# A two-layer attention and mixture kernel: the first norm applied by ScalarE, two narrow matmul groups made 128 columns wide, and a new order of each engine's work within a body

## The chip, the cores and the metric

One NeuronCore of a Trainium2 chip runs the kernel. The metric is the device time in microseconds (us) of one execution; the kernel before took 1501.69 us (median of 3 runs, 1501.0 to 1501.98). A core has five engines with an instruction stream each, which meet only through semaphores: TensorE (PE; its weight loads are PEld), VectorE (DVE), ScalarE (ACT), GpSimd (POOL) and SyncE (SP), which here only issues DMAs.

## The reference

The input is x of 16 batches x 512 tokens x 128 features, in float32. In short:

```python
x = x + linear_attention(norm(x))        # "layer 1": q, k, v of 16 heads of 8; Chebyshev terms of order 1 to 5 of
                                         # clipped q, k; running sums over tokens; numerator / denominator; W_out
y = norm(x)
y = y + causal_softmax_attention(norm(y) * g1 + b1)     # "layer 2"
y = y + top2_of_8_experts(norm(y) * g2 + b2)            # gate logits = h @ gate_W + gate_b
out = x + y
norm(x) = (x - mean) / sqrt(var + 1e-5)                 # over the 128 features of a token
den = (Tq.sum(-1) * k_beta).sum(orders)                 # one denominator per token and head
```

## The kernel before, in words

A batch (512 tokens, four tiles of 128) is one unit of work. Layer 1, layer 2's projections, the row maxima of the softmax, the scores with the values, and the gate are five stages of a software pipeline. `pipelined` (L306) calls a `body` 21 times on each engine, with up to six batches in flight: f (first norm, projections and Chebyshev terms), h (running sums, denominators, output of layer 1), g (projections of layer 2), m (row maxima), b (scores, exponentials, values) and t (gate and dispatch of rows to the experts). Body -5 has only f, body -4 f and h, body -3 adds g, body -2 adds m, body -1 adds b, and bodies 0 to 10 have all six. Then the stages fall away again (f first, then h), until body 15 has t alone. Behind the last body come 39 blocks of expert work (L1589 to L1599), which the change doesn't touch.

Within a body every engine's order is written out by hand. Each of DVE, ACT and PE runs through 129 numbered slots. Long runs of equal work have lists of slots: row maxima on PE (`MAX_PE`, 44 in a body, `maximum`, L1362) and on DVE (`MAX_DVE`, L583), scores on PE (`SCORES_PE`, 48, L1400) and their exponentials on ACT (`EXPS_ACT`, L966), value matmuls (`VALUES_PE`, 12, L1419). Every other step has one slot (`at(n, stage)`). A slot is only a place in that engine's own order; it is no time. POOL's order stands in its own `body` (L1188) without slots.

Two rings tie the engines: a score matmul may run at most two ahead of the exponentials (L1407), and a maximum matmul at most two ahead of DVE's reductions (L1370). All waits are in order, so what stands behind a waiting instruction on its engine waits too.

The steps that the change touches:

- **The first norm.** `stats0` (DVE, slot 0, L506) writes mean and variance; `ln_rsqrt("a", f)` (POOL, L1193 calling L412) makes 1/sqrt; `apply0` (DVE, slot 23, L461) writes `hn = (x - mean) * rstd` as four 128x128 instructions; `turn_h` (PE, slot 61) transposes it; `take_h` (ACT, slot 40) copies it to `hT`; `project_k` and `project_q` (PE, slots 68 and 69, both on L1277) use it.
- **The other norms.** ACT applies them with scale and shift (`ln_shift`, L455): `apply3` (slot 10), `apply1` (73), `apply2` (77). For those POOL makes a shift, -mean * rstd, in two more steps (L427, L428) and a last one (L444).
- **The denominators.** `denominators` (PE, slot 32, L1310): four matmuls of float32 with a 128x128 stationary operand and 16 moving columns. `invert_den` on DVE (slot 18) adds epsilon and inverts, and `turn_rden` (PE, slot 47) transposes.
- **The gate.** `gate` (PE, slot 33, L1467): four matmuls of float32 with 8 moving columns, then `gate_top` (DVE, slot 25), `gate_exp` (ACT, 28), `gate_weights` (DVE, 28), `ranks` (PE, 58), `slots` (DVE, 34), and POOL's eight indirect DMAs (`dispatch`, L1176).
- **Layer 2's projections.** `turn_ln` (PE, slot 43), `affine1` (ACT, 26), `project_q2` (PE, 51, L1351), `project_k2` (PE, 52, L1354), `project_v2` (55, L1359).
- `copy_rows` (ACT, slot 12, L993) copies the normed rows; `set_tables` (DVE, body -5 only) fills constant tables.

The profile counts one float32 matmul as two PE instructions.

Of the kernel before, what the change touches and what calls it, by code (L numbers as in the profile page):

```python
# [22 lines left out]
ALU = mybir.AluOpType  # L23
# [88 lines left out]
def block_kernel(nc, x, consts, cols, row_biases, w_in, w_out, wq, wk, wv, wp, gate_w, ew1, ew2, eb2, out):  # L112
    with ExitStack() as ctx:
# [90 lines left out]
        for c in "amb":  # L204
# [84 lines left out]
        MAX_PE = (1, 2, 7, 8, 11, 13, 20, 23, 38, 41, 44, 49, 53, 54, 57, 60, 62, 65, 67, 71, 73, 75, 77, 79, 85, 88, 89, 93, 94, 99, 102,  # L289
                  106, 107, 110, 112, 114, 116, 117, 119, 120, 122, 123, 124, 126)  # L290
        SCORES_PE = (0, 5, 6, 10, 12, 14, 16, 17, 18, 19, 21, 24, 26, 27, 29, 30, 31, 34, 36, 37, 39, 40, 42, 46, 48, 50, 56, 59, 64, 66,
                     70, 78, 80, 84, 86, 90, 92, 95, 97, 98, 101, 104, 105, 108, 109, 111, 113, 115)
        VALUES_PE = (15, 22, 28, 35, 45, 63, 76, 87, 96, 103, 118, 121)
        MAX_DVE = (1, 2, 6, 7, 9, 11, 19, 20, 22, 24, 26, 27, 29, 30, 31, 32, 33, 35, 38, 40, 42, 44, 47, 48, 51, 54, 55, 58, 59, 61, 62,
                   64, 65, 66, 67, 68, 69, 70, 71, 72, 73, 74, 75, 77)
        EXPS_ACT = (0, 1, 2, 3, 4, 5, 6, 7, 8, 9, 11, 13, 15, 16, 18, 19, 20, 21, 22, 23, 24, 25, 27, 29, 31, 32, 37, 39, 42, 45, 49, 54,
                    56, 58, 59, 61, 62, 63, 65, 66, 67, 68, 69, 70, 71, 72, 74, 75)
        LEAVE_ACT = (17, 43, 64)
        SPLIT_DVE, SPLIT_ACT = (6, 10, 15, 20), (8, 9, 11, 15, 30, 32, 34, 36)
# [112 lines left out]
        def ln_rsqrt(c, n):  # L412
# [43 lines left out]

        def ln_apply(c, n, src, dst):
            k = norm[c]
            nc.vector.wait_ge(k["ready"], n + 1)
            for t in range(QT):  # L460
                nc.vector.tensor_scalar(dst(t), src(t), k["mv"][:, t, 0:1], k["rstd"][:, t:t + 1],  # L461
                                        ALU.subtract, ALU.mult).then_inc(k["out"], 1)
# [3 lines left out]
        def _(dve):  # L466
# [42 lines left out]

            def apply0(f):  # L510
                ln_apply("a", f, tile_of(f), lambda t: hn[:, t, :])
# [160 lines left out]
            def body(t, b, m, g, h, f, p):  # L672

                for n in range(SLOTS):
# [7 lines left out]
                    if at(3, t):  # L682
                        x2(t)
# [6 lines left out]
                    if at(10, h):  # L690
                        times_v(h, (0, 1))
                    if at(12, h):
                        sum_kv(h, (0,))
                    if at(13, h):
# [9 lines left out]
                    if at(18, h):  # L704
                        invert_den(h)
                    if at(21, h):
                        sum_kv(h, (4,))
                    if at(23, f):
                        apply0(f)
                        if f == 0:  # L710
                            set_tables()
# [6 lines left out]
                    if at(36, g):  # L718
                        third_part(g, 2, kf, ks)
                    if at(37, g):  # L720
                        third_part(g, 1, qf, qs)
                    if at(39, f):
                        clip(f, kx, W.hk_ev, W.k_clip)
                    if at(41, f):
                        clip(f, qx, W.hq_ev, W.q_clip)
                    if at(43, b):
# [899 lines left out]
```

## Time and profile before

| | |
|---|---|
| median of 3 runs | 1501.69 us |
| the profiled execution's own time | 1503.87 us |
| its span (first to last instruction) | 1501.6 us, 27731 instructions |
| mean granted TensorE clock | 0.907 |
| busy: PE, DVE, ACT, POOL | 1261.9, 1152.0, 912.0, 847.7 us |
| chain that ended last | PE 64%, DVE 15%, ACT 8%, issue 5%, DMA 3%, POOL 3% |
| of it `hn` by DVE, L461 | 3% |
| largest waits | ACT L972 for PE L1415 199.0 us; PEld L1412 for ACT L972 123.7 us; DVE L587 for PE L1375 95.5 us |

The profiled execution took 2.3 us more than its span, and 2.2 us more than the median. The span falls into four parts: five bodies that fill the pipeline (to about 231 us), the eleven full bodies (to about 928 us, some 63 us each), five bodies that drain it (to about 1180 us) and the expert blocks. "Granted clock" is the share of TensorE's full clock of 2.4 GHz that the throttle let through; its two levels are 1.00 and 0.50. "Idle before, with a releaser" means that the engine did nothing for that long and that the named instruction's semaphore ended it.

### The profile page before, as it was taken

Reading aid. Unit: us, or ns where it says so; the run is one execution under the profiler, and the core shown is the slowest. Engines: PE = TensorE matmul, PEld = TensorE weight load, DVE = VectorE, ACT = ScalarE, POOL = GpSimd, SP = SyncE. Lnnn points to the kernel's source line nnn. Section 1 sums busy time; section 2 is a strip of 40 time slices with the busy share of each in tenths; the row PEclk is TensorE's granted clock in tenths of the full one; section 3 lists DMA queues with packets and bytes.
Section 4 is the critical chain, followed back from the end, with each engine's and each line's share of the span. In section 5 each row is a group of like instructions: output and inputs, shape, how many; then the busy total and the mean of one; then the engine's idle time right before and its main releaser. Section 6 shows DMA issues by size and latency. Waiting matters only on the chain.

```text
span 1501.6 us, 27731 instructions
## 1 busy us (share of the span) xinstructions
PE 1261.9 (84%) x8819; PEld 734.1 (49%) x8819; DVE 1152.0 (77%) x2622; ACT 912.0 (61%) x1795; POOL 847.7 (56%) x1077
## 2 busy tenths in 40 slices
PE   3466898999999999899998999988886399999970
PEld 1233254554545445454454544544343288888750
DVE  5658888888988888888988888856541588888765
ACT  1233376676756766567665766674564488888760
POOL 5776545667666676666767666532213246666570
PEclk8567799999999999999999999998998599999995
DMA  3032121422224222242321413223033212222238
GB/s 98 0 84 64 22 76 22 111 64 53 75 41 108 72 51 72 44 108 64 60 72 37 97 37 83 72 44 94 23 121 141 75 51 76 86 80 79 67 118 352
DMA packets 79344, 116.22 MB, mean 77 GB/s; under 512 B 15396, under 2 KB 61496, under 8 KB 74976
## 3 DMA queue, kind: packets, MB, share of 16 engines
q1 hardware_dynamic: 65888, 92.41, 23.7%
q0 software_dynamic: 9088, 17.33, 3.4%
q10 hardware_dynamic: 4224, 4.72, 0.9%
q8 instruction: 71, 1.16, 0.3%
q14 instruction: 73, 0.60, 0.1%
HBM read 58.29 MB, written 57.43 MB: 77 GB/s over the span
## 4 chain that ended last, share of the span: by engine, by line
PE 64%; DVE 15%; ACT 8%; issue 5%; DMA 3%; POOL 3%; another core or an unknown queue 1%; SPq 0%; POOLq 0%; DVEq 0%; ACTq 0%
PE back L1432 8%; PE scores L1412 8%; PE maxima L1373 8%; DVE nm L587 7%; PE front L1565 7%; PE back L1577 6%; PE front L1302 4%; PE maxima L1375 3%; DVE hn L461 3%; ACT pr L972 3%; PE front L1277 3%; PE scores L1415 2%; PE back L1252 2%; ACT rows L455 2%; DMA stack<-pairs 2%
## 5 line engine op out<-in xcount | busy, mean ns | idle before, releaser
L972 ACT ACTIVATE pr<-scores 128x384 f32<-128x384 f32 (+1 forms) x768 | 382.2, 525 | 232.0 <-PE scores L1415 199.0
L587 DVE TENSOR_REDUCE nm<-maxima 128x1 f32<-128x384 f32 (+3 forms) x704 | 426.7, 635 | 107.7 <-PE maxima L1375 95.5
L1412 PE MATMUL scores<-stack 98*128 98x512 bf16 (+3 forms) x1024 | 271.0, 314 | 32.7 <-ACT pr L972 29.8
L1373 PE MATMUL maxima<-stack 96*128 96x128 bf16 (+3 forms) x1024 | 258.0, 313 | 41.7 <-DVE nm L587 39.6
L1176 POOL DMA_INDIRECT xg<-rows,sloti x128 | 133.3, 1042 | 111.2 <-DVE sloti L657 71.4
L1412 PEld LDWEIGHTS scores<-stack 98*128 98x128 bf16 x1024 | 94.0, 102 | 197.6 <-ACT pr L972 123.7
L1415 PE MATMUL scores<-maskB,identb 128*128 128x128 bf16 (+1 forms) x768 | 189.0, 246 | 0.0
L1432 PE MATMUL back<-pr,vaug 128*9 128x512 f32 (+3 forms) x2048 | 182.5, 452 | 0.0
L1375 PE MATMUL maxima<-maskA,identb 128*128 128x128 bf16 (+2 forms) x704 | 177.4, 252 | 0.0
L1373 PEld LDWEIGHTS maxima<-stack 96*128 96x128 bf16 x1024 | 90.1, 100 | 170.1 <-DVE nm L587 81.3
L1241 POOL DMA_INDIRECT pairs<-xs x104 | 105.8, 1017 | 92.4 <-DVE xs L822 65.0
L1565 PE MATMUL front<-h_first,w_now 128*128 128x512 f32 x312 | 129.2, 415 | 6.2 <-ACT xs L1111 3.0
L1111 ACT ACTIVATE xs<-front,b1p 128x512 f32<-128x512 f32 x156 | 107.3, 688 | 32.2 <-PE front L1565 20.6
L1146 POOL TENSOR_TENSOR kv<-F,kv 128x512 f32<-128x512 f32 x80 | 107.1, 1360 | 12.4 <-DVE kv L541 12.2
L1137 POOL TENSOR_SCALAR F<-F 128x512 f32<-128x512 f32 x32 | 56.7, 1772 | 72.7 <-DVE F L520 71.2
L1577 PE MATMUL back<-hid_first,w_now 128*128 128x512 f32 x312 | 97.1, 393 | 0.0
L541 DVE TENSOR_TENSOR_SCAN kv<-one,front 128x512 f32<-128x512 f32 x80 | 93.5, 1201 | 0.0
L815 DVE TENSOR_TENSOR hid_second<-xs,hid_first 128x512 fp32r<-128x512 f32 x99 | 68.0, 687 | 28.2 <-ACT hid_first L1092 26.5
L1157 POOL TENSOR_TENSOR kv<-kv 128x512 f32<-128x512 f32 x64 | 81.0, 1275 | 3.8 <-POOL kv L1157 0.4
L1415 PEld LDWEIGHTS scores<-maskB,identb 128*128 128x128 bf16 x768 | 77.3, 101 | 11.4 <-issue 4.0
L1092 ACT ACTIVATE hid_first<-xs 128x512 fp32r<-128x512 f32 x117 | 74.0, 633 | 3.7
L1167 POOL TENSOR_TENSOR qf<-qf,qs 128x512 f32<-128x512 f32 x16 | 18.5, 1156 | 100.2 <-ACT qs L922 100.2
(222 smaller groups left out, 2542.5 us busy)
## 6 DMA issues: line engine op xcount, KB each, us to landing
stack<-spread SPq DMA_DIRECT2D x64, 384.0 KB
spread<-qs SPq DMA_DIRECT2D x96, 128.0 KB
spread<-ks SPq DMA_DIRECT2D x96, 128.0 KB
xs<-xg SPq DMA_DIRECT2D x39, 272.0 KB
stack<-pairs SPq DMA_DIRECT2D x8, 1024.0 KB
xg<-xs SPq DMA_DIRECT2D x17, 272.0 KB
xs<-in_x SPq DMA_DIRECT2D x16, 256.0 KB
acc<-xs SPq DMA_DIRECT2D x16, 256.0 KB, 2.3
```

Source lines behind the costliest of these rows:

```text
L587: v.tensor_reduce(nm[:, h:h + heads, t], ring(n)[:, 0:heads * (t + 1) * P].rearrange("p (h n) -> p h n", h=heads), AX.X, ALU.max, negate=T ...
L972: a.activation(pr[:, n % PR, 0:width], ringE[n % 2][:, 0:width], ACT.Exp).then_inc(W.exp_ready, 1)
L1111: a.activation(gel[n % GS], (X, Y)[n % 2][:, :], ACT.Gelu, bias=b1p[:, bass.ds(ahead * HC + c, 1)]).then_inc(W.mid_ready, 1)
L1146: g_.tensor_tensor(kv[:, p, :], qx[p], kv[:, p, :], ALU.mult).then_inc(W.qk_prod, 1)
L1176: g_.indirect_dma_start(xg[:, :], bass.IndirectOffsetOnAxis(sloti[:, i, q:q + 1], 0), rows[:, i, q, :], None).then_inc(W.dispatched, 16)
L1373: k.matmul(ring(n)[:, at:at + (t + 1) * P], qst[p][0:MROW, h, t * P:(t + 1) * P], kst[p][0:MROW, h, 0:(t + 1) * P], start=(j == 0), stop=T ...
L1375: k.matmul(ring(n)[:, 0:heads * (t + 1) * P].rearrange("p (h n) -> p h n", h=heads)[:, :, t * P:(t + 1) * P], identb[:, :], maskA[:, 0:hea ...
L1412: k.matmul(dst[:, at:at + T - t * P], kst[p][0:MROW + 2, h, t * P:(t + 1) * P], qst[p][0:MROW + 2, h, t * P:T], start=(t == tiles[0]), sto ...
L1415: k.matmul(dst[:, 0:2 * P * many].rearrange("p (i n) -> p i n", i=many)[:, :, 0:P], identb[:, :], maskB[:, 0:many * P].rearrange("p (i n) ...
L1432: last = k.matmul(V[32 * i:32 * i + DH + 1, t * P:T], vaug[:, b % VR, t, 4 * (s_ // 3) + i, :], pr[:, (4 * s_ + i) % PR, at:at + T - t * P ...
L1565: last = k.matmul((X, Y)[n % 2][:, :], w_now[:, i % 2, wi, c * P:(c + 1) * P], h2p[hi][:, i % 2, :], start=(j == 0), stop=(j == len(TERMS3 ...
L1577: last = k.matmul((Z, V)[i % 2][:, :], w_now[:, i % 2, 2 + wi, c * P:(c + 1) * P], (hidh, hidl)[hi][i % 2 * HC + c], start=(c == 0 and j = ...
```

## The change

DVE no longer applies the first norm; ACT does, by `ln_shift`, for which POOL makes the shift in norm "a" too. The denominators and the gate write 128 columns per tile, of which the first 16 or 8 are used (each tile overwrites the surplus of the one before). `project_k`'s wait is on another semaphore where g is absent. All slots are chosen anew, and on POOL `dispatch(t, 0, (3,))` stands ahead of the even orders of q, and `ln_rsqrt("m", h)` behind `dispatch(t, 1, (1,))`.

```diff
-        LEAVE_ACT = (17, 43, 64)
-        SPLIT_DVE, SPLIT_ACT = (6, 10, 15, 20), (8, 9, 11, 15, 30, 32, 34, 36)
+        LEAVE_ACT = (20, 45, 66)
+        SPLIT_DVE, SPLIT_ACT = (6, 10, 15, 20), (8, 9, 11, 32, 35, 37, 39, 41)
...
-            steps = first + (shifted if c != "a" else []) + (second if c == "m" else [])
+            steps = first + shifted + (second if c == "m" else [])
...
-                if c != "a" and i + 1 == len(first) + len(shifted):
+                if i + 1 == len(first) + len(shifted):
                     g.tensor_tensor(shift, minus, rstd, ALU.mult).then_inc(k["ready"], 1)
-            if c == "a":
-                g.tensor_tensor(rstd, y0, a, ALU.mult).then_inc(k["ready"], 1)
...
DVE body
                     if at(0, f):
                         stats0(f)
+                        if f == 0:
+                            set_tables()
-                    if at(3, t):
+                    if at(1, t):
                         x2(t)
...
-                    if at(21, h):
-                        sum_kv(h, (4,))
-                    if at(23, f):
-                        apply0(f)
+                    if at(18, h):
+                        sum_kv(h, (4,))
+                    if at(19, h):
+                        invert_den(h)
...
-                    if at(28, t):
+                    if at(27, t):
                         gate_weights(t)
-                    if at(34, t):
+                    if at(32, t):
                         slots(t)
...
ACT body
+            def apply0(f):
+                act.wait_ge(norm["a"]["ready"], f + 1)
+                ln_shift("a", tile_of(f), lambda t: hn[:, t, :], False)
...
-                    if at(12, t):
-                        copy_rows(t)
-                    if at(14, t):
+                    if at(13, t):
                         affine2(t)
+                    if at(16, f):
+                        apply0(f)
-                    if at(26, g):
+                    if at(28, h):
+                        take_rden(h)
+                    if at(29, g):
                         affine1(g, t)
-                    if at(28, t):
+                    if at(31, t):
+                        copy_rows(t)
+                    if at(33, t):
                         gate_exp(t)
-                    if at(30, h):
-                        take_rden(h)
...
-                    if at(60, m):
+                    if at(64, m):
                         put_maxima(m, p, 0)
-                    if at(73, h):
+                    if at(77, h):
                         apply1(h)
-                    if at(77, h):
+                    if at(78, h):
                         apply2(h, g)
-                    if at(80, m):
+                    if at(81, m):
                         put_maxima(m, p, 1)
...
POOL body
                     dispatch(t, 0, (2,))
+                    dispatch(t, 0, (3,))
                 if f is not None:
                     even_orders(f, qx, W.q_t35, W.q_t24)
-                if t is not None:
-                    dispatch(t, 0, (3,))
-                if h is not None:
-                    ln_rsqrt("m", h)
                 if t is not None:
                     dispatch(t, 1, (0,))
                     dispatch(t, 1, (1,))
                 if h is not None:
+                    ln_rsqrt("m", h)
                     keep_residual(h)
...
PE body
-                    last = k.matmul(X[:, t * H:(t + 1) * H], ksum[:, t * P:(t + 1) * P], cst[:, C_WS:C_WS + H],
+                    last = k.matmul(X[:, t * H:t * H + P], ksum[:, t * P:(t + 1) * P], cst[:, C_WS:C_WS + P],
                                     start=True, stop=True)
...
-                    last = k.matmul(Z[:, t * E:(t + 1) * E], h2[:, t * P:(t + 1) * P], gw_sb[:, :], start=True, stop=True)
+                    last = k.matmul(Z[:, t * E:t * E + P].rearrange("p (i n) -> p i n", n=E), h2[:, t * P:(t + 1) * P],
+                                    gw_sb[:, :].unsqueeze(1).to_broadcast((P, P // E, E)), start=True, stop=True)
...
-                    if at(33, t):
+                    if at(37, t):
                         gate(t)
-                    if at(43, g):
+                    if at(42, g):
                         turn_ln(g, h)
-                    if at(47, h):
+                    if at(44, h):
                         turn_rden(h)
...
-                    if at(68, f):
+                    if at(66, f):
                         project_k(f, h, g)
-                    if at(69, f):
+                    if at(71, f):
                         project_q(f)
-                    if at(74, f):
+                    if at(77, f):
                         project_v(f)
...
```

## Rows read from the trace of the kernel before

**Rows 1.** Busy us per engine, granted clock: the sum over the eleven bodies, 246.9 to 943.8.
```profile
sum 696.90, PE 654.59 PEld 346.26 DVE 605.09 ACT 461.17 POOL 466.20; mean PE 59.51 PEld 31.48 DVE 55.01 ACT 41.92 POOL 42.38
```
**Rows 2.** Timeline of PE (start us, us, instructions): denominators and the next project_k.
```profile
246.87 1.01 PE L1310 MATMUL front<-cst,ksum 128*128 128x16 f32 x8
...
625.04 1.01 PE L1310 MATMUL front<-cst,ksum 128*128 128x16 f32 x8
...
643.90 1.93 PE L1277 MATMUL front<-hT,w_in_sb 128*128 128x512 f32 x4
...
834.71 1.93 PE L1277 MATMUL front<-hT,w_in_sb 128*128 128x512 f32 x4
...
879.11 1.01 PE L1310 MATMUL front<-cst,ksum 128*128 128x16 f32 x8
...
943.84 1.04 PE L1310 MATMUL front<-cst,ksum 128*128 128x16 f32 x8
```
**Rows 3.** The chain that ended last, in order of time, 624 to 644.
```profile
629.72 3.08 DVE hn L461 x4
...
635.53 1.81 PE front L1351 x2
637.34 1.48 PE front L1354 x2
```
**Rows 4.** Timeline of PE: waits in that stretch, and layer 2's projections in four bodies.
```profile
258.20 1.07 PE L1351 MATMUL front<-lnT,wq_sb 128*128 128x512 f32 x2
...
573.63 1.07 PE L1351 MATMUL front<-lnT,wq_sb 128*128 128x512 f32 x2
574.54 1.02 PE L1354 MATMUL front<-lnT,wk_sb 128*128 128x512 f32 x2
...
633.45 0.40 PE L1373 MATMUL maxima<-stack 96*128 96x128 bf16 x4 [0.66 <-DVE nm L587]
...
634.91 0.51 PE L1412 MATMUL scores<-stack 98*128 98x512 bf16 x1 [0.84 <-ACT pr L972]
...
953.48 1.07 PE L1351 MATMUL front<-lnT,wq_sb 128*128 128x512 f32 x2
```
**Rows 5.** Busy time by stretch: PE, PEld, DVE, ACT, POOL, then PE's granted clock.
```profile
559.90:563.40 3.50, 2.94 (x35) 1.87 (x26) 2.42 (x4) 2.84 (x6) 3.50 (x4) 0.99 0.00 0
563.40:570.20 6.80, 6.80 (x33) 3.49 (x34) 4.67 (x8) 2.39 (x5) 6.58 (x6) 0.50 0.00 0
...
635.00:638.40 3.40, 3.40 (x6) 1.40 (x6) 2.04 (x10) 1.77 (x4) 0.00 (x0) 0.51 0.01 2
```
**Rows 6.** Groups of instructions by form: count, busy us, mean ns of one, idle before.
```profile
L461 DVE TENSOR_SCALAR hn<-xs,mva,rstda 128x128 f32<-128x128 f32 x64 | 52.2, 875 | 5.5 <-POOL rstda L446 5.5
...
L455 ACT ACTIVATE rows<-x2t,moreb,rstdb 128x128 f32<-128x128 f32 x64 | 26.2, 482 | 5.6 <-POOL moreb L444 5.6
...
L993 ACT ACTIVATE rows<-rows 128x512 f32<-128x512 f32 x16 | 9.9, 620 | 0.0
```
**Rows 7.** The same view: matmuls of 16 and of 128 columns on 128x128 stationary operands.
```profile
L1310 PE MATMUL front<-cst,ksum 128*128 128x16 f32 x128 | 18.8, 281 | 22.0 <-DVE kv L541 22.0
...
L1359 PE MATMUL front<-wv_sb,lnT 128*128 128x128 f32 x128 | 17.7, 284 | 0.0
```
**Rows 8.** Timeline of ACT just behind the denominators of body 6.
```profile
627.22 0.49 ACT L972 ACTIVATE pr<-scores 128x384 f32<-128x384 f32 x1 [1.49 <-PE scores L1415]
```
**Rows 9.** Timeline of POOL: last steps of norm "b", and of norm "a" behind it.
```profile
617.60 0.20 POOL L427 TENSOR_TENSOR rstdb<-lnvb 128x4 f32<-128x4 f32 x1
...
618.34 0.20 POOL L444 TENSOR_TENSOR moreb<-moreb,rstdb 128x4 f32<-128x4 f32 x1
...
621.85 0.20 POOL L446 TENSOR_TENSOR rstda<-lnva 128x4 f32<-128x4 f32 x1
```
**Rows 10.** Timeline of PE in bodies -4 and -2: waits that end with or behind hn.
```profile
45.62 1.11 PE L1252 MATMUL front<-cst,hn 128*128 128x128 f32 x4 [5.58 <-DVE hn L461]
...
131.68 0.61 PE L1373 MATMUL maxima<-stack 96*128 96x128 bf16 x4 [3.54 <-DVE nm L587]
```

More of the change, by code:

```diff
@@ L455, in ln_shift @@
                 nc.scalar.activation(dst(t), src(t), ACT.Identity, bias=bias[:, t:t + 1], scale=scale[:, t:t + 1]).then_inc(k["out"], 1)
[L457 to L462, printed above, removed]
         @block.vector
@@ L691, in body @@
                         times_v(h, (0, 1))
+                    if at(11, h):
+                        sum_kv(h, (0,))
                     if at(12, h):
-                        sum_kv(h, (0,))
-                    if at(13, h):
                         sum_kv(h, (1,))
@@ L1039, in body @@
                         take_k(f, h)
-                    if at(46, f):
+                    if at(48, f):
                         take_q(f, h)
-                    if at(47, f):
+                    if at(49, f):
                         square(f, kx, W.k_clip, W.k_sq)
-                    if at(48, f):
+                    if at(50, f):
                         square2(f, kx, W.k_sq)
-                    if at(50, f):
+                    if at(51, f):
                         square3(f, kx, W.k_sq)
-                    if at(51, f):
-                        take_v(f, h)
                     if at(52, f):
                         square(f, qx, W.q_clip, W.q_sq)
-                    if at(53, f):
+                    if at(54, f):
+                        take_v(f, h)
+                    if at(55, f):
                         square2(f, qx, W.q_sq)
-                    if at(55, f):
+                    if at(57, f):
                         square3(f, qx, W.q_sq)
-                    if at(57, m):
+                    if at(59, m):
                         max_parts(m, 0)
-                    if at(60, m):
+                    if at(64, m):
                         put_maxima(m, p, 0)
-                    if at(73, h):
-                        apply1(h)
                     if at(76, b):
@@ L1064, in body @@
                     if at(77, h):
+                        apply1(h)
+                    if at(78, h):
                         apply2(h, g)
-                    if at(78, m):
+                    if at(79, m):
                         max_parts(m, 1)
-                    if at(79, b):
+                    if at(80, b):
                         take_y(b)
-                    if at(80, m):
+                    if at(81, m):
                         put_maxima(m, p, 1)
@@ L1494, in body @@
                         head_sums(h, kx, X, W.k_t24, W.k_t35, W.ks_mm, W.x1_ready, h)
-                    if at(9, h):
+                    if at(10, h):
                         head_sums(h, qx, Y, W.q_t24, W.q_t35, W.qs_mm, *((W.x2_ready, t + 1) if t is not None else (W.outT_ready, h)))
-                    if at(25, t):
+                    if at(24, t):
                         turn_x2(t)
@@ L1526, in body @@
                         spread_rden(h, g, f)
-                    if at(82, b):
+                    if at(82, m):
+                        turn_maxima(m, b, 0)
+                    if at(86, b):
                         turn_back(b, 1, t)
-                    if at(83, m):
-                        turn_maxima(m, b, 0)
-                    if at(91, h):
+                    if at(93, h):
                         output1(h, g, f)
-                    if at(100, b):
+                    if at(102, b):
                         turn_back(b, 2, t)
-                    if at(125, b):
+                    if at(124, b):
                         turn_back(b, 3, t)
```

82 lines of the change are left out of this document (39 added, 43 removed).

## The prediction

> **What bounds the kernel now.** I read four views in turn. First the busy time by stretch: in the eleven bodies between the first and the last denominators with all stages around them, PE is busy 654.59 of 696.90 us and DVE 605.09, ACT and POOL only 461.17 and 466.20 [rows 1]. PE is the bound, and DVE stands close behind it. Second, PE's timeline at two marks of a body, the start of the denominators and that of `project_k`. From `project_k` to the next denominators PE takes 44.40 us (879.11 less 834.71), and in the other bodies the same to 0.1. The mean period is (943.84 - 246.87) / 11 = 63.36 us [rows 2]. So the whole variation, and as I shall argue most of the loss, lies in the stretch from denominators to `project_k`: 63.36 - 44.40 = 18.96 us on average. Third, the chain of waits in one such stretch: `hn` on DVE stands in it with 3.08 us in one piece, and behind it come `project_q2` and `project_k2` with 1.81 and 1.48 us [rows 3]. Fourth, the clock. At the full clock such a pair takes 0.91 us from start to start [rows 4]; in this body both ran at 0.51 of the clock, the level of 1.2 GHz [rows 5].
>
> **The stretch without its losses.** In body 6 it took 643.90 - 625.04 = 18.86 us [rows 2]. PE waited 0.66 us for DVE's reduction, which stood behind `hn`, and 0.84 us for ACT [rows 4]; ACT had to sit out DVE's gate work, which stood behind `hn` too. The two pairs cost 1.81 + 1.48 - 2 x 0.91 = 1.47 us too much through the clock [rows 3, 4]. What PE needs by itself is 18.86 - 1.50 - 1.47 = 15.9 us. In body 5 the clock fell right behind denominators and gate, for 6.8 us, without much waiting before it: PE was busy 2.94 of the 3.50 us ahead [rows 5], with the narrow groups as its last work. So the loss has two sources, a wait behind `hn` or narrow matmuls ahead of a fall, and the change goes at both.
>
> **`hn` leaves DVE.** Four instructions a body, 64 x 875 ns = 52.2 us in all [rows 6]. The cleanest look at its worth is the first body without f: there `project_q2` starts 953.48 - 943.84 = 9.64 us behind the denominators, in the body at 246.87, with gate and DVE's `hn` and the same single fall of the clock, 11.33 us [rows 2, 4]. That is 1.7 us a body from DVE alone, though 3.1 us leave it: PE takes over as bound for the rest.
>
> **`hn` comes to ACT.** 4 x 482 ns = 1.9 us a body at most, and `copy_rows`, 0.62 us, moves from ahead of it to a later slot [rows 6]. So ACT's work ahead of the denominators grows by 1.3 us net, with exponentials behind it for which PE's scores wait. Behind the denominators ACT was idle for 1.49 us in one piece [rows 8], which is the cover. The ring of two scores lets part of it through: between nothing and 1.3 us a body I take 0.3, near the lower end because ACT's cover is larger than the growth. PE's `turn_h` is late in the order and has no reason to wait.
>
> **POOL's shift.** Norm "a" gets two more small steps; for norm "b" they take 618.34 - 617.60 = 0.74 us [rows 9]. The result comes at 622.05 + 0.74 = 622.8 instead. ACT reaches slot 16 at about that time, so I charge nothing in full bodies; POOL's products behind it start 0.7 us later, hidden by POOL's idle third [rows 1]. Without that cover it would be 0.7 us a body.
>
> **Denominators and gate wide.** Eight float32 matmuls a body. A group of 16 columns has a mean of 281 ns an instruction, one of 128 columns 284 [rows 7]; 16 instructions a body cost 0.05 us. The Trainium skill, in "TensorE: Matmul & The Clock Gate", Back-to-back issue gap, has the gap grow with the moving columns, at the full clock by 112 / 2.4 = 47 ns for 112 columns more. An estimate from that page is 0.75 us a body, some 9 us in all, and the forecast would be as much higher; the rows show instead that these groups take what their weights take. What the width gives is the clock. If it stays up behind the groups, the stretch loses its second source too. The trace of before can't show this. Its bounds are nothing, and the whole difference between a stretch of 18.96 - 1.7 = 17.3 and one of 15.9 us.
>
> **The moves.** The last running sum (DVE) goes ahead of `invert_den`, into DVE's wait for PE; `turn_rden` and ACT's copy are needed only at `project_q2` and later. The gate moves four slots back on PE and `gate_exp` five on ACT, so that exponentials stand no more behind DVE's gate work. Maxima and scores are interleaved otherwise; I take their effect as zero between -1 and +1 us a body. `ln_rsqrt("m")` goes behind two more indirect DMAs of POOL, and both `apply1` and `apply2` behind the third evacuation on ACT, before `take_y`; the two small DMAs of `put_maxima` move back by a few slots and are wanted only by the next body's scores. `set_tables` goes ahead of POOL's result, where DVE idled.
>
> **The sum.** For a body I take 15.9 us plus 0.5 for waits that remain or come new = 16.4 us, so 18.96 - 16.4 = 2.6 less, and 0.3 back for ACT: 2.3 us. Twelve bodies (the eleven, and body -1) give 27.6. Filling the pipeline: in body -4 PE stood 5.58 us for `hn`, in body -2 3.54 us for the reduction behind it [rows 10]; I take 4.0 and 3.5, less 0.7 for POOL's steps in body -3 and 1.2 for these and ACT's slower `hn` in body -5: 5.6. The body at 943.84 has the narrow groups alone: 0.8. Together 34 us. Against the profiled execution, 1503.9, that is 1469.9; against the median of the runs, which is 2.2 lower, **1468 us**.
>
> **Rivals.**
> - *The clock stays as it is*, only DVE's share comes: 12 x (1.7 - 0.3) + 5.6 = 22 us, **1479**. For it: PE was hardly idle before the fall at 563.4 [rows 5], so it isn't plain that wider matmuls help. The Trainium skill, same page, Part 1, ties the throttle to idleness of PE; by that rule widening busy work would do nothing, and this rival would be the result. The row of 2.94 busy of 3.50 with a fall behind it speaks against idleness as the only cause. Chance 0.22.
> - *The rest of the body gets shorter too.* PE is idle or its releases late for (696.90 - 654.59) / 11 = 3.8 us a body [rows 1], some 2.3 of it outside the stretch. If the new order takes 1.2 of that and my charges of 0.3 fall away, 12 x 1.5 = 18 us more: **1450**. Chance 0.15.
> - *Slower: ACT waits for POOL in `apply0`.* Slot 16 stands ahead of exponentials, and these ahead of PE's scores. POOL gets to norm "a" only behind norm "b" [rows 9], and to that behind the indirect DMAs of the body before, of which two more now hold up `ln_rsqrt("m")` and with it the residual. If the result comes w us later than ACT is there, PE loses w - 1.5, ACT's cover taken off [rows 8]. Against a gain of 2.3 us it decides from w = 3.8 a body; at w = 5 twelve bodies lose 14 us net, less 6 of the filling: **1510**. Against it: POOL's busy share is only 67% [rows 1], and `stats0` stays at slot 0. Chance 0.08.
> - *Nothing:* a wait of 2 to 3 us takes the place of `hn` (ACT's tail, two norms ahead of `take_y`): 1501. Chance 0.05.
>
> **How the numbers follow.** The forecast has 0.50, from 1458 to 1478 (2.3 us a body with 0.8 either way). With the first rival and most of the second the range is 1450 to 1490. A measurement of this kernel can tell about 0.2%, 3 us. Faster by more: 0.50 + 0.22 + 0.15 = 0.87; within: 0.05; slower: 0.08.
>
> **What would show it.** Periods between denominators of 60.5 to 61.5 us; denominators to `project_k` in 16 to 17 us; no stretch at the half clock right behind the denominators; L461 gone from DVE, 64 more of L455 on ACT at 0.48 us; `turn_h` of body -4 some 4 us earlier. It would be wrong if the half clock shows up as often, if `project_k` to denominators takes more than 45 us, or if ACT stands idle for POOL's L444 in full bodies.

## The result, and the profile after

| | before | changed |
|---|---|---|
| median of the runs | 1501.35 us (4 runs) | 1484.1 us (1480.95 to 1487.06, 4 runs) |
| ratio, 95% interval | | 0.9889 (0.9864 to 0.9913) |
| span of the profiled execution | 1501.6 us | 1481.8 us |
| granted clock, whole span | 0.907 | 0.922 |

The change gained 17 us; I had forecast 33 to 34. The range held it, the number did not. A second measurement, in a later set of runs, gave 1484.55 us and a ratio of 0.9903 (0.9867 to 0.9939). The page of the changed kernel (share of the span and count behind each busy time; then the chain that ended last):

```profile
span 1481.8 us, 27795 instructions
...
PE 1243.5 (84%) x8819; PEld 730.9 (49%) x8819; DVE 1107.9 (75%) x2558; ACT 942.3 (64%) x1859; POOL 864.5 (58%) x1109
...
PE 61%; POOL 9%; issue 9%; ACT 9%; DVE 7%; DMA 3%; another core or an unknown queue 1%; POOLq 0%; SPq 0%; ACTq 0%; DVEq 0%
```

DVE's share of the chain fell from 15% to 7%. The marks of the body [rows 2], on PE's timeline of the changed kernel (start, duration, instructions):

```profile
180.92 1.71 PE L1300 MATMUL front<-cst,ksum 128*128 128x128 f32 x8
...
241.46 1.11 PE L1300 MATMUL front<-cst,ksum 128*128 128x128 f32 x8
...
608.47 1.11 PE L1300 MATMUL front<-cst,ksum 128*128 128x128 f32 x8
...
623.11 1.07 PE L1267 MATMUL front<-hT,w_in_sb 128*128 128x512 f32 x2
...
915.00 1.13 PE L1300 MATMUL front<-cst,ksum 128*128 128x128 f32 x8 [0.40 <-DVE kv L529]
```

The mean period is (915.00 - 241.46) / 11 = 61.23 us, in place of 63.36. In body 6 the stretch from denominators to `project_k` took 623.11 - 608.47 = 14.64 us, in place of 18.86; the rest of the body, from `project_k` to the next denominators, grew from 44.4 us to 46.6 (61.23 - 14.64). The windows (PE, PEld, DVE, ACT, POOL busy, then the granted clock) of the first 3.4 us of that stretch, and of one of the three short falls that are left in the full bodies [rows 5 in the kernel before]:

```profile
608.40:611.80 3.40, 3.40 (x30) 2.18 (x29) 1.96 (x5) 2.55 (x6) 3.40 (x4) 1.00 0.02 5
...
484.60:488.00 3.40, 3.06 (x14) 2.38 (x14) 1.31 (x3) 1.98 (x5) 3.40 (x4) 0.56 0.00 0
```

The groups by form [rows 6 and 7]: the new `hn` on ACT, the denominators and the gate.

```profile
L453 ACT ACTIVATE hn<-xs,morea,rstda 128x128 f32<-128x128 f32 x64 | 26.2, 482 | 36.8 <-POOL morea L444 36.8
...
L1300 PE MATMUL front<-cst,ksum 128*128 128x128 f32 x128 | 23.8, 345 | 19.2 <-DVE kv L529 19.2
...
L1457 PE MATMUL back<-gw_sb,lnT 128*128 128x128 f32 x128 | 18.7, 291 | 0.9 <-ACT lnT L974 0.9
```

ACT waited 36.8 us for POOL's L444, all of it in bodies -5 to -2 and none in a full body, the largest piece in body -4:

```profile
36.99 1.65 ACT L453 ACTIVATE hn<-xs,morea,rstda 128x128 f32<-128x128 f32 x4 [16.11 <-POOL morea L444]
```

**Where the time came from and where it went**, in the two profiled executions: up to the denominators of body -1 the kernel won 3.24 us (184.16 to 180.92), in the twelve bodies from there to body 11 another 25.6 (759.7 to 734.1), and from the denominators of body 11 to the end it lost 9.0 (557.8 to 566.8). The sum is the 19.8 us between the spans; by the medians it is 17. I call bodies 11 to 15, in which no batch enters any more, the drain, and mark it by `output2`, the matmuls with which PE opens stage t of a body. The loss begins at once: from output2 of body 11 to that of body 15 the changed kernel takes 233.1 us, the kernel before 228.2.

### The profile page after: what moved, and what is told of

Its sections match the earlier page's. It is cut to its first block, busy times and chain, and to the rows that moved or that the text cites. A ratio compares the mean times of both kernels' runs of the same rounds, so it can differ in the third digit from the quotient of the medians.

```text
span 1481.8 us, 27795 instructions
## 1 busy us (share of the span) xinstructions
PE 1243.5 (84%) x8819; PEld 730.9 (49%) x8819; DVE 1107.9 (75%) x2558; ACT 942.3 (64%) x1859; POOL 864.5 (58%) x1109
## 4 chain that ended last, share of the span: by engine, by line
PE 61%; POOL 9%; issue 9%; ACT 9%; DVE 7%; DMA 3%; another core or an unknown queue 1%; POOLq 0%; SPq 0%; ACTq 0%; DVEq 0%
PE scores L1402 8%; PE back L1422 8%; PE front L1556 7%; PE back L1568 6%; PE maxima L1363 6%; PE front L1292 4%; PE scores L1405 3%; DVE nm L575 2%; PE maxima L1365 2%; PE front L1267 2%; ACT pr L962 2%; POOL xg L1168 2%; PE back L1242 2%; DMA stack<-pairs 2%; POOL F L1130 1%
## 5 line engine op out<-in xcount | busy, mean ns | idle before, releaser
L1402 PE MATMUL scores<-stack 98*128 98x512 bf16 (+3 forms) x1024 | 259.0, 307 | 38.7 <-ACT pr L962 27.5
L1168 POOL DMA_INDIRECT xg<-rows,sloti x128 | 144.1, 1126 | 107.9 <-DVE sloti L645 72.5
L1402 PEld LDWEIGHTS scores<-stack 98*128 98x128 bf16 x1024 | 90.1, 98 | 199.3 <-ACT pr L962 108.1
L1405 PE MATMUL scores<-maskB,identb 128*128 128x128 bf16 (+1 forms) x768 | 185.0, 241 | 0.0
L1422 PE MATMUL back<-pr,vaug 128*9 128x512 f32 (+3 forms) x2048 | 178.7, 445 | 0.4 <-ACT oT L966 0.4
L1365 PEld LDWEIGHTS maxima<-maskA,identb 128*128 128x128 bf16 x704 | 70.2, 100 | 12.6 <-issue 8.6
```

Of the source, the lines that this page charges most:

```text
L1168: g_.indirect_dma_start(xg[:, :], bass.IndirectOffsetOnAxis(sloti[:, i, q:q + 1], 0), rows[:, i, q, :], None).then_inc(W.dispatched, 16)
L1365: k.matmul(ring(n)[:, 0:heads * (t + 1) * P].rearrange("p (h n) -> p h n", h=heads)[:, :, t * P:(t + 1) * P], identb[:, :], maskA[:, 0:hea ...
L1402: k.matmul(dst[:, at:at + T - t * P], kst[p][0:MROW + 2, h, t * P:(t + 1) * P], qst[p][0:MROW + 2, h, t * P:T], start=(t == tiles[0]), sto ...
L1405: k.matmul(dst[:, 0:2 * P * many].rearrange("p (i n) -> p i n", i=many)[:, :, 0:P], identb[:, :], maskB[:, 0:many * P].rearrange("p (i n) ...
L1422: last = k.matmul(V[32 * i:32 * i + DH + 1, t * P:T], vaug[:, b % VR, t, 4 * (s_ // 3) + i, :], pr[:, (4 * s_ + i) % PR, at:at + T - t * P ...
```

## The experiments

### Each part by itself, and all but the order

The old order with the wide groups alone:

```diff
-                    last = k.matmul(X[:, t * H:(t + 1) * H], ksum[:, t * P:(t + 1) * P], cst[:, C_WS:C_WS + H],
+                    last = k.matmul(X[:, t * H:t * H + P], ksum[:, t * P:(t + 1) * P], cst[:, C_WS:C_WS + P],
```

and the gate likewise.

> The kernel before with the denominators and the gate 128 columns wide, and nothing else of the change. Theory A (the widening is what holds the clock): the half-clock stretches right behind the denominators, one in nearly every full body before, go; my prediction put the clock at 11 us of its 33, so about 1490 us. Theory B (the clock fell because PE stood idle for hn, whatever the columns): the stretches stay and the time is 1500 to 1503 us.

Measured: 1505.3 us, ratio 1.0035 (1.0018 to 1.0052): slower, if anything. Theory A has the clock right and the time wrong; theory B has it the other way round, near enough. Windows of body 4 of this experiment, behind the denominators, and PE's waits later in that stretch:

```profile
502.70:506.10 3.40, 3.40 (x31) 2.25 (x30) 2.23 (x6) 1.20 (x3) 3.40 (x3) 1.00 0.00 0
506.10:509.50 3.40, 3.32 (x31) 1.74 (x29) 3.40 (x4) 2.46 (x6) 3.32 (x4) 1.00 0.00 0
```

```profile
512.31 0.40 PE L1373 MATMUL maxima<-stack 96*128 96x128 bf16 x4 [1.76 <-DVE nm L587]
...
513.77 0.39 PE L1412 MATMUL scores<-stack 98*128 98x512 bf16 x1 [0.84 <-ACT pr L972]
```

The clock stays up right behind the denominators, in this and in every full body. But PE now stands 1.76 us for the reduction behind `hn`, where it stood 0.66 us in body 6 of the kernel before [rows 4]: the faster PE waits longer for DVE. Two things make the mean stretch even longer than before. Six full bodies have a fall of 3 to 4 us some 11 us behind the denominators, and their stretch takes 19.8 to 20.2 us, where the others take 17.4 to 18.4. And DVE's `hn` itself takes longer, 62.9 us in all against 52.2 [rows 6]:

```profile
L461 DVE TENSOR_SCALAR hn<-xs,mva,rstda 128x128 f32<-128x128 f32 x64 | 62.9, 1042 | 8.5 <-POOL rstda L446 8.5
```

Why it does isn't shown. In body -5 of the kernel before, with POOL idle, the four instructions took 1.12 us; in body -4, with POOL busy for 4.9 us of them, 5.07 us.

The old order with `hn` on ACT alone; the added lines stand in ACT's body, the first removed one in DVE's, and `project_k` waits as in the change:

```diff
+                    if at(16, f):
+                        apply0(f)
...
                     if at(23, f):
-                        apply0(f)
                         if f == 0:
                             set_tables()
...
-                    pe.wait_ge(W.d_prod, h + 1)
+                    pe.wait_ge(W.kv_sum, h * ORDERS + ORDERS)
```

> The kernel before with hn written by ACT from the scale and shift (at ACT's place 16, with POOL's one more operation), narrow denominators and gate and every engine's old order; project_k waits for the last order's sum of keys and values, as in the change. Theory A: the way from the denominators to project_k shortens by 1.5 to 2.5 us a body, but half clock stays in most bodies: about 1480 us. Theory B (idle time makes the clock fall): the half-clock stretches go with the wait for hn, and it reaches 1475 us or less. If ACT's four operations delay exps as much as they free DVE: 1495 to 1502 us.

Measured: 1497.8 us, ratio 0.9982 (0.9968 to 0.9996), which is the time of the third forecast: ACT's operations delay as much as they free, 1.25 us off the stretch and 1.5 us on the rest of the body in the table below. Theory B falls: PE has no wait left in the stretch, and half clock in its stead: from 619.0 to 627.0, right behind the denominators of body 6,

```profile
619.00:627.00 8.00, 8.00 (x43) 4.64 (x43) 4.30 (x8) 2.39 (x5) 7.12 (x6) 0.57 0.01 2
```

Both together, without the new order:

> Everything of the change but the new order: hn on ACT (place 16), wide denominators and gate, every engine's old order. Widening alone took the half clock behind the denominators away and gave nothing, hn on ACT alone gave 2 us and kept half clock. Theory E (each is worth nothing alone, as hn's path and the slow PE end in the same wait; together they give the stretch back): the bodies run at 60.5 to 61.5 us and the whole at 1470 to 1478 us. Theory F (the bodies need the new order, the old one only moves the wait into the rest of the body): periods stay at 62 to 63 us, 1488 to 1497 us.

Measured: 1478.6 us, ratio 0.9823 (0.9772 to 0.9874; the kernel before took 1507.9 us beside it). Theory E holds for the period, and the time is at the upper end of its range. The denominators of body 6 and 7 stand at 608.07 and 669.39, a period of 61.32 us:

```profile
608.07 1.11 PE L1311 MATMUL front<-cst,ksum 128*128 128x128 f32 x8
...
623.47 1.93 PE L1278 MATMUL front<-hT,w_in_sb 128*128 128x512 f32 x4
...
669.39 1.11 PE L1311 MATMUL front<-cst,ksum 128*128 128x128 f32 x8
```

So the full bodies owe the new order next to nothing, and the whole kernel is no slower without it (ratios 0.9823 and 0.9889, whose intervals touch).

### Taking one part out of the changed kernel

> The changed kernel with the denominators 16 and the gate 8 columns wide as before. Theory A: half clock is back behind the denominators in most full bodies, 0.6 to 1.1 us a body, so 1491 to 1496 us. Theory B: the clock stays as in the changed kernel (three short falls in the full bodies) and the time is 1484 us.

Measured: 1512.1 us, ratio 1.0063 (1.0041 to 1.0085), 28 us more than the change by the medians, 26 by the ratios: more than either theory allowed. Seven of the eleven full bodies fell to half clock for some 10 us and took 64.3 to 65.7 us; the other four took 60.4 to 60.8, and each of them follows one that fell. Windows of 11 us ahead of and behind the denominators, in bodies 5 (first pair) and 6:

```profile
549.70:560.70 11.00, 8.87 (x75) 3.70 (x75) 10.96 (x14) 9.35 (x21) 8.96 (x18) 0.98 0.07 19
...
560.70:571.70 11.00, 11.00 (x59) 7.11 (x61) 3.39 (x8) 4.32 (x11) 8.52 (x7) 0.56 0.00 0
...
614.80:625.80 11.00, 8.87 (x76) 3.70 (x75) 10.97 (x14) 9.24 (x21) 8.96 (x18) 1.00 0.08 24
...
625.80:636.80 11.00, 11.00 (x90) 7.14 (x89) 7.40 (x32) 8.74 (x20) 8.65 (x7) 1.00 0.01 2
```

What PE did ahead of the two is the same, 8.87 us of 11; one falls, the other doesn't. These rows don't say what decides. With 128 columns, PE busy 8.88 us of the 11 ahead of body 6 too, the clock stays:

```profile
597.40:608.40 11.00, 8.88 (x74) 3.63 (x74) 10.96 (x15) 9.16 (x21) 8.96 (x17) 1.00 0.08 24
```

`hn` back on DVE, at its place 23, the rest of the change kept:

> The changed kernel with hn written by DVE again (at DVE's old place 23), its new order and wide columns kept. Theory G (hn's path on DVE is what bound the old bodies): the stretch from the denominators to project_k is 18 us again, periods 63 to 64 us, 1505 to 1515 us. Theory H (the order alone shortened it): periods 61 to 62 us, below 1492 us.

Measured: 1527.6 us, ratio 1.0157 (1.0102 to 1.0213). Theory G holds, and more: the stretch is 20.0 us, and the four operations stand in the way with more than 4 us (1049 ns each, as with the wide groups alone). Ten of the eleven full bodies also have a fall of the clock late in the stretch, from 13 or 17 us behind the denominators.

```profile
634.96 4.20 DVE L507 TENSOR_SCALAR hn<-xs,mva,rstda 128x128 f32<-128x128 f32 x4
...
641.46 1.63 PE L1354 MATMUL front<-wv_sb,lnT 128*128 128x128 f32 x8 [1.15 <-ACT qf L911]
```

A summary from PE's timelines and the windows. The period is the mean of the twelve from body -1 to body 11; the stretch, the rest and the idle time (the time less PE's busy time in it) are means of bodies 1 to 7. "Half clock" is the time at 1.2 GHz between 240 and 920 us: twice what the granted clock lacks to 1, summed over windows of 1 us. The medians come from several chips; the kernel before took 1507.9 us beside the fourth and the last kernel, and 1500 to 1501.4 beside the others.

| kernel | median | ratio | period | stretch | idle PE in it | rest | idle PE in it | half clock |
|---|---|---|---|---|---|---|---|---|
| before | 1501 | 1 | 63.31 | 18.72 | 0.96 | 44.43 | 2.67 | 58 |
| wide | 1505 | 1.0035 | 63.38 | 19.43 | 2.61 | 44.43 | 2.67 | 21 |
| `hn` on ACT | 1498 | 0.9982 | 63.09 | 17.47 | 0.00 | 45.95 | 4.20 | 58 |
| both, old order | 1479 | 0.9823 | 61.28 | 15.40 | 0.14 | 45.94 | 4.36 | 1 |
| changed | 1484 | 0.9889 | 61.17 | 15.02 | 0.00 | 46.30 | 3.83 | 10 |
| changed, narrow | 1512 | 1.0063 | 63.44 | 17.04 | 0.00 | 46.29 | 3.83 | 72 |
| changed, `hn` on DVE | 1528 | 1.0157 | 64.03 | 20.03 | 3.09 | 44.68 | 2.37 | 48 |

The means hide how the two limits hide each other; the single stretches of the four kernels with the old order show it. With `hn` on DVE a fall right behind the denominators costs 0 to 0.6 us, with `hn` on ACT it costs 1.2 to 2.9 us:

| fall right behind the denominators | stretch, `hn` on DVE | stretch, `hn` on ACT |
|---|---|---|
| none | 18.35 us (wide, bodies 0 and 4) | 15.40 us (both, bodies 1 to 7) |
| 3 to 4 us | 18.33 and 18.34 us (before, bodies 0, 2, 8) | 16.6 to 16.7 us (bodies 0, 2, 5, 7, 9) |
| some 7 us | 18.6 to 18.9 us (before, bodies 1, 3, 5, 7) | 18.0 to 18.3 us (the other six) |

### The 1.5 us in the rest of the body

The table's rest grows by 1.5 us in every kernel with `hn` on ACT. In the kernel with both parts and the old order, ACT and PE just ahead of the denominators at 608.07 (timelines of ACT and of PE):

```profile
605.16 1.65 ACT L453 ACTIVATE hn<-xs,morea,rstda 128x128 f32<-128x128 f32 x4
606.69 0.60 ACT L975 ACTIVATE oT<-back 128x512 f32<-128x512 f32 x1
607.17 1.59 ACT L971 ACTIVATE pr<-scores 128x512 f32<-128x512 f32 x3
```

```profile
607.83 0.34 PE L1413 MATMUL scores<-stack 98*128 98x384 bf16 x1 [2.04 <-ACT pr L971]
```

PE's scores wait 2.04 us for exponentials that stand behind `hn` (0.53 us at that place with the wide groups alone). In the kernel with both parts and the old order, the experiment moves `hn` into the time behind the denominators in which ACT waits for PE:

```diff
-                    if at(16, f):
-                        apply0(f)
+                    if at(20, f):
+                        apply0(f, (0, 1))
+                    if at(21, f):
+                        apply0(f, (2,))
+                    if at(23, f):
+                        apply0(f, (3,))
```

> As the run with hn on ACT, wide columns and the old order, but ACT writes hn in three pieces, at its places 20 (two tiles), 21 (one) and 23 (one), in place of four tiles at place 16. Theory J (in the rest of the body the moved operations cost 1.5 us, since PE's scores right ahead of the denominators wait 2.05 us for the exps that stand behind hn): that wait goes, the operations fall into ACT's own idle time behind the denominators, and the bodies take 59.5 to 60.3 us, 1459 to 1468 us in all against a before of 1500. Theory K (PE's 57 us of work and its other waits take that time back elsewhere): 61 to 61.5 us a body and the same time as with one piece.

Measured: 1424.1 us against a before of 1469.9 on this chip, ratio 0.9679 (0.9627 to 0.9731); and once more, on another chip:

> The kernel with ACT's hn in three pieces a second time, with POOL's transfers in an unbroken run. Full bodies of 59.9 us each again (against 61.2 in the changed kernel), so 20 to 25 us faster than the changed kernel of this call, of which 14 to 16 in the full bodies; its drain as said for the kernel beside it.

Measured: 1457.7 us, ratio 0.9721 (0.9684 to 0.9758). Theory J holds on both, with a gain a little beyond its range. In the second run a full body takes 59.92 us (59.85 by the table's count), the rest is back at 44.43 and the idle PE in it at 2.67 us, and no full body falls to half clock. ACT's `hn` in the second run, just behind the denominators at 596.94, and PE's wait ahead of the next ones:

```profile
597.52 0.87 ACT L944 ACTIVATE hn<-xs,morea,rstda 128x128 f32<-128x128 f32 x2
...
601.26 0.49 ACT L944 ACTIVATE hn<-xs,morea,rstda 128x128 f32<-128x128 f32 x1
```

```profile
656.62 0.34 PE L1421 MATMUL scores<-stack 98*128 98x384 bf16 x1 [0.53 <-ACT pr L975]
656.86 1.11 PE L1319 MATMUL front<-cst,ksum 128*128 128x128 f32 x8
```

This is the fastest kernel of the study: 26.9 us less than the changed one beside it (1484.55), where 20 to 25 were expected.

### The drain

> The changed kernel, but in the four bodies of the drain (no first stage left) all engines follow the order of before. Theory C (the new order is what costs the drain its 6 to 9 us: scores 31 and 32 stand ahead of the sixth group of values there, and ACT stands for them): output2 of bodies 12 to 15 keeps the lead of 28 us that it has in body 12, and the time is 1476 to 1478 us. Theory D (POOL's unbroken run of indirect transfers delays ACT and DVE, in whatever order): the stalls of 4 to 7 us on ACT stay and the time is 1482 to 1486 us.

Edit: each engine's `body` of before is kept beside the new one and called where f is absent, with the old lists of slots. Measured: 1475.6 us, ratio 0.9839 (0.9812 to 0.9866), the time of theory C. A second run of it, beside the unaltered changed kernel:

> The changed kernel, unaltered, beside the three others of this call on one chip. Against the same before: 17 us faster, as measured at first, if what the drain gives back is the order's; from output2 of body 11 to that of body 15 it takes 5 to 9 us more than the kernel with the old order there.

> The kernel with the old order in the bodies without a first stage, a second time, beside the changed kernel. If the order costs the drain 6 to 9 us, it is that much faster than the changed kernel here too; if its lead in the first run was the chip's, the two are within 2 us.

Measured: 1484.55 and 1480.2 us, ratios 0.9903 (0.9867 to 0.9939) and 0.9878 (0.9841 to 0.9914); these intervals overlap, and the medians differ by 4.4 us. The two profiles show where: output2 of bodies 11 and 15 in the changed kernel, then in the one with the old drain.

```profile
900.45 1.16 PE L1447 MATMUL front<-wp_sb,hn 128*128 128x128 f32 x8 [0.46 <-ACT hn L970]
...
1135.00 2.08 PE L1447 MATMUL front<-wp_sb,hn 128*128 128x128 f32 x8 [0.69 <-ACT hn L970]
```

```profile
899.40 1.16 PE L1670 MATMUL front<-wp_sb,hn 128*128 128x128 f32 x8 [0.95 <-ACT hn L1066]
...
1125.28 1.16 PE L1670 MATMUL front<-wp_sb,hn 128*128 128x128 f32 x8 [0.69 <-ACT hn L1066]
```

234.5 against 225.9 us, and 233.1 against 226.1 in the earlier pair, whose kernels did not run beside each other: 7 to 9 us for the new order. That is the high end. Of the four executions of each kernel, the ones profiled for these rows were the slowest of the changed kernel and the fastest of the other, and three more profiles with the old order in the drain and the same two parts have 228.1, 229.2 and 230.0 us. So the new order costs the drain something between 3 and 9 us, and the 4.4 between the medians on one chip are the least selected figure.

> The changed kernel; in the bodies without a first stage alone the seventh group of values stands at place 74, ahead of scores 31 and 32, in place of 80. Theory C1 (this one exchange is what costs the drain its time, since the exps of scores 32 wait for the buffer that this group frees): ACT's stalls of 5.4, 6.8 and 4.4 us go, the drain takes 5 to 8 us less, 1476 to 1479 us. Theory C2 (another part of the order: the stages' places on PE, DVE's or POOL's order): 1482 to 1486 us.

Measured: 1488.5 us, ratio 0.9887 (0.9838 to 0.9937), and 241.6 us for the drain. C1 falls: the drain is longer with the exchange.

> The changed kernel; in the bodies without a first stage PE and ACT follow the order of before, DVE and POOL the new one. From output2 of body 11 to that of body 15 the kernels with the new order took 233.1 us, those with the old one 226 to 230 us. If PE's and ACT's order costs the drain its time: 226 to 230 us; if DVE's does: 233 us.

> The changed kernel; in the bodies without a first stage DVE alone follows the order of before. If DVE's order costs the drain its time, the stretch from output2 of body 11 to that of body 15 takes 226 to 230 us; if PE's and ACT's does, 233 us; if the engines' orders only fit together as a set, more than 233 us in one of these two kernels.

These two have one execution each, 1452.0 and 1447.5 us on the chip on which before took 1469.9. Their drains took 215.9 and 212.4 us. That can't be set against 233 or 226, as this chip runs bodies 12 to 14 faster (below); with the old order on all engines it took 205.7. Only body 11 takes the same on every chip. From output2 of body 11 to that of body 12:

| order in the drain | body 11 |
|---|---|
| old on all engines (four kernels with both parts) | 58.3 us |
| new on all engines | 60.9, 61.0 us |
| old on PE and ACT only | 60.1 us |
| old on DVE only | 60.2 us |
| new, seventh group of values earlier | 63.6 us |

Either half gives 0.7 to 0.9 us of the 2.7, both together all of it. The orders fit as a set; no single exchange was found that accounts for the loss. In body 11 the cost of the new order, 2.7 us, is firm.

> The changed kernel with every engine in the old order in the five bodies of the filling and in the five of the drain, and in the new order only in the eleven full bodies. The drain gives 8 us as in the run before; in the filling the old order with hn on ACT reached the denominators of body 3 (by the stage's own count) at 177.0 us, the new order at 180.9 us. If that lead is kept: 1471 to 1473 us, the fastest of all. If the change of order between the bodies costs it again: 1475 to 1477 us.

Measured: 1478.9 us, ratio 0.9824 (0.9774 to 0.9875), the same as both parts with the old order throughout, and above both forecasts: its drain took 229.2 us, not 226. The denominators of body -1 (its stage h is at batch 3, hence the expectation's "body 3") came at 178.4 us: the lead was partly kept, and is too small to tell in the whole.

> The kernel with ACT's hn in three pieces; besides, in the bodies without a first stage POOL waits behind each of its eight indirect transfers until it has landed. On the chip of the first traces all engines stood 7.7 us longer in body 12 (from 34 to 48 us behind output2) than on the chip of the last call, in the same order, and this began under POOL's run of transfers at 28.8 to 38.8 us. Theory D (the unbroken run makes the other engines stand): this kernel's drain takes 206 us on either chip. If the run is not the cause: the same time as the kernel with the run unbroken, 226 to 230 us on a chip like the first, 206 on one like the last.

The kernel is the one with `hn` in three pieces. Edit: behind each indirect transfer of bodies 11 to 15 POOL waits for its landing. Measured: 1486.8 us, ratio 0.9916 (0.9894 to 0.9939), 29 us slower than with the run unbroken (1457.7, beside it). The drain took 232.6 us in place of 228.1, and the time from output2 of body 15 to the end 373.0 in place of 350.2. By the time neither forecast holds for the whole. But the trace shows that the stalls did go. In bodies 12 to 14 ACT's waits for which the profile names no engine of this core ("issue" or "remote") sum up to some 21 us with the run unbroken, the longest 5.15 us. With the transfers held apart they are some 3 us, the longest 1.08, and on the chip that took 1424.1 us the same with the run unbroken. What takes their place is ACT waiting for POOL, whose shift now stands behind the landings: 19.3 us in the same bodies, and 17.8 in body 15 in place of 5.6. In body 12, ACT with the transfers apart:

```profile
953.98 1.65 ACT L453 ACTIVATE rows<-x2t,moreb,rstdb 128x128 f32<-128x128 f32 x4 [5.82 <-POOL moreb L444]
...
979.93 1.10 ACT L975 ACTIVATE pr<-scores 128x384 f32<-128x384 f32 x2 [3.72 <-PE scores L1426]
```

So theory D has the stalls for it and the time against it, because holding POOL up costs as much as the stalls did. That the run of transfers takes part in the stalls on this chip follows from this one profile; that a cheaper way of breaking it would save time is not shown.

## Why the prediction was right or wrong

**The stretch** (forecast 16.4 us): 15.02. The mechanism was right, with `hn` off DVE and the clock up behind the denominators in all but three full bodies; the 0.5 us for waits that remain was not needed, and neither was all of the 15.9 for PE.

**The sources as a sum.** I gave DVE's share 1.7 us a body by itself, from the first body without f, and let the clock come on top; the first rival had 1479 us by it. In the table `hn` on ACT alone shortens the stretch by 1.25 us, and the rest takes 1.5 back; the wide groups alone lengthen it by 0.7; both together shorten it by 3.3. With `hn` on DVE the stretch ends by DVE, almost whatever the clock (18.33 to 18.35 us with and without a fall of 3 to 4 us); with `hn` on ACT and narrow groups it ends by a PE at half clock. The 1.47 us that I had put down to the clock in body 6 were too much too: bodies 4 and 6, with that late fall, took 18.85 us where bodies 0, 2 and 8 took 18.34. The sum of both was right, the split was not, and by the first rival's arithmetic `hn` alone would have given 22 us where it gave about 3.

**ACT** (forecast 0.3 us, bound 1.3): 1.5 in the old order, 1.9 in the new. This term was mis-sized beyond its bound, and one of my own signs of being wrong came with it: the rest of the body takes 46.3 us, more than 45. I set ACT's idle 1.49 us [rows 8] against the four operations as cover; but that idle time lies behind the denominators, and place 16 lies ahead of them, where exponentials that PE waits for are next. Cover at another place of the order is no cover. With `hn` moved to where it is, the whole 1.5 us came back. In the full bodies this error and the one on the stretch offset each other: 2.14 us a body (25.6 / 12) against 2.3.

**Filling** (forecast 5.6 us): 3.2. `turn_h` of body -4 came 45.62 - 41.59 = 4.03 us earlier, as forecast:

```profile
41.59 1.09 PE L1242 MATMUL front<-cst,hn 128*128 128x128 f32 x4 [0.45 <-ACT rdT L886]
...
79.97 2.08 PE L1341 MATMUL front<-lnT,wq_sb 128*128 128x512 f32 x2 [6.11 <-ACT lnT L893]
```

But body -3 gave all of it back, not 0.7: the denominators of body -2 start at 121.31 in both traces. Its `project_q2` stood 6.11 us for ACT's `lnT`. What was kept is body -2's.

**POOL's shift, the widening's own price, the slower rival.** No wait for L444 in a full body: POOL's two steps cost nothing there, and the rival at 1510 us is out. The wide denominators took 1.11 us for eight instructions in place of 1.01 at full clock, 0.10 a body where I had 0.05. The gate's eight went from 1.04 to 1.11. The estimate from the Trainium skill ("TensorE: Matmul & The Clock Gate", Back-to-back issue gap) was 0.75 us a body, and an estimate by the same section's table, which gives up to 64 columns one and the same cost, would be some 0.5; the trace bears neither out for these groups. Part 1 of the same page of the Trainium skill ties the clock to how busy PE has been. By that, widening busy work would do nothing; the trace doesn't agree: with the new order, 16 and 8 columns had 72 us of half clock where 128 had 10, with PE busy 8.87 and 8.88 of the 11 us ahead.

**The moves and the drain: the step that failed.** "I take their effect as zero between -1 and +1 us a body" was applied to the full bodies alone, where it holds (0.1 us). For all that follows the forecast had 0.8 us of gain, for body 11. The new order costs the drain 3 to 9 us against the old one, 2.7 of it in body 11 alone; I had not worked through a body without f. Of the 9.0 us lost against the kernel before behind body 11's denominators, 4.9 lie between the output2 marks. A further 3.8 lie behind the last one (346.0 to 349.8 us); among kernels with the same code there it ranged from 345.6 to 352.9 on two of the chips, so I don't put it down to the change. The cause of the order's cost within the drain stays open: it is the order as a whole, and no single step of it was found.

In sum: 2.4 us are missing in the filling, 2.0 in the full bodies, 9.8 behind them; the drain's order is the largest part of the last that an experiment shows. The order, a third of the change's text, was worth nothing in the full bodies and cost what it cost at the end.

## What to carry to other kernels

When two limits end the same stretch (here an engine's queue and PE's clock), removing either alone can show almost nothing, so a part's worth has to be tested with the other gone too. Idle time covers moved work only at that place in the engine's order; look at what stands behind the new place and who waits for it. An experiment that removes a wait and costs time elsewhere should be read at the wait, not by its total. An order tuned for the steady state should be priced for the bodies that fill and drain a pipeline too, and may be kept separate there.

## What the hardware showed that I had not expected

Widening matmuls by columns that are thrown away kept the clock up: time at half clock went from 58 to 21 us, from 58 to 1 and from 72 to 10 in three pairs of kernels that differ in nothing else. In the last pair the narrow groups had a fall in seven of eleven bodies, for some 10 us and at a cost of some 5 us each, where the wide ones had three of 3 to 4 us. Why the width does it isn't shown. And in the bodies at the end one chip differs from the others. The kernel with `hn` in three pieces took 1457.7 us on one chip and 1424.1 on another. Of the 37.0 us between the two spans 22.4 lie between output2 of body 11 and that of body 15 (228.1 and 205.7), and another 13.1 behind that (350.2 and 337.1), in the last body and the expert blocks. In body 12 both run alike up to 33 us behind output2; then the first chip's engines stand (timelines of ACT in the first and in the second run, at the same place of the order):

```profile
972.33 0.49 ACT L975 ACTIVATE pr<-scores 128x384 f32<-128x384 f32 x1 [4.49 <-issue]
974.46 0.49 ACT L975 ACTIVATE pr<-scores 128x384 f32<-128x384 f32 x1 [1.64 <-PE scores L1424]
...
980.68 1.13 ACT L975 ACTIVATE pr<-scores 128x384 f32<-128x384 f32 x2 [1.39 <-PE scores L1424]
```

```profile
970.13 1.10 ACT L975 ACTIVATE pr<-scores 128x384 f32<-128x384 f32 x2 [3.73 <-PE scores L1424]
971.56 1.10 ACT L975 ACTIVATE pr<-scores 128x384 f32<-128x384 f32 x2
```

POOL's unbroken run of transfers takes part in it: with a wait behind each, these stalls were gone on the first chip, at a cost elsewhere (above). Why they come on one chip and not on the other is open. The granted clock, 0.64 from 980 to 986 in the first and 1.00 in the second, is no cause of the first stalls, as it was 1.00 there from 968 to 973.
